# The loops of an attention and of two feed-forward passes written out, with every wait on a constant

## The reference

```python
# feed-forward: 8 experts of width 64, two picked per token, and a shared one of width 128
g = silu(einsum('th,ehi->tei', xf, w_gate))
u = einsum('th,ehi->tei', xf, w_up)
experts_y = einsum('tei,eih->teh', g * u, w_down)
...                                   # the two picked ones, weighed
shared = silu(x @ sw_gate) * (x @ sw_up) @ sw_down

# attention: 16 heads of 8 channels, power 4 of the scores in place of a softmax
s = einsum('bhtd,bhsd->bhts', q, k)
s = s - s.mean(-1)
s = s / (abs(s).mean(-1) + 1e-06) * score_gain
s = where(causal, s, -1000.0)
r = maximum(s, 0.0) ** 4
att = r / (r.sum(-1) + 1e-06)
y = einsum('bhts,bhsd->bhtd', att, v)
```

## Time and profile before

| what | us |
|---|---|
| runs | 505.57, 505.78, 507.81; median 505.78 |
| span of the profiled execution, first to last instruction (the profile gives no other time of it) | 505.4 |
| TensorE busy | 441.9 (87%) |
| VectorE busy | 402.7 (80%) |
| ScalarE busy | 342.0 (68%) |
| GpSimd busy | 243.8 (48%) |

### The profile page before, as it was taken

The page is one execution under the profiler, slowest core; times in us unless marked ns, Lnnn a source line. Parts: engine busy times, 40 slices in busy tenths (PEclk is TensorE's granted clock), DMA queues, the critical chain, the costliest instruction groups (busy, mean ns, idle before and its releaser), DMA issues. The chain is left out here.

```text
span 505.4 us, 8943 instructions
## 1 busy us (share of the span) xinstructions
PE 441.9 (87%) x2736; PEld 168.3 (33%) x2736; DVE 402.7 (80%) x832; ACT 342.0 (68%) x576; POOL 243.8 (48%) x180
## 2 busy tenths in 40 slices
PE   0879999664799999999999999999999995879996
PEld 0323444431232332333333322323323354334442
DVE  5884556976898998999989899989988969784443
ACT  3413223554999999999999999999989931523221
POOL 5940000333777686776877677676876720000000
PEclk9979999975999999999999999999999998799999
DMA  4300000025714205105114124043002300000001
GB/s 118 75 1 0 1 0 0 6 65 127 208 33 78 60 1 95 43 1 93 42 30 71 34 51 84 0 72 63 0 0 50 85 12 0 1 1 0 21 21 42
DMA packets 17796, 21.32 MB, mean 42 GB/s; under 512 B 4748, under 2 KB 10476, under 8 KB 17772
## 3 DMA queue, kind: packets, MB, share of 16 engines
q1 hardware_dynamic: 17452, 20.95, 19.2%
q10 hardware_dynamic: 320, 0.07, 0.1%
HBM read 13.02 MB, written 7.86 MB: 41 GB/s over the span
## 5 line engine op out<-in xcount | busy, mean ns | idle before, releaser
L1206 POOL TENSOR_TENSOR arena<-arena 128x1024 f32<-128x1024 f32 (+1 forms) x120 | 204.0, 1722 | 63.7 <-ACT arena L1178 63.5
L1136 DVE SCALAR_TENSOR_TENSOR arena<-bank,masks 128x1024 f32<-128x1024 f32 (+1 forms) x160 | 174.9, 1114 | 28.9 <-PE bank L1048 28.6
L1178 ACT ACTIVATE arena<-arena 128x1024 f32<-128x1024 f32 (+1 forms) x160 | 148.5, 961 | 8.8 <-DVE arena L1136 5.8
L1048 PE MATMUL bank<-Q,K 128*128 128x512 bf16 (+3 forms) x384 | 91.4, 334 | 10.6 <-DMA K<-k_parts 9.2
L1048 PE MATMUL bank<-K,Q 128*128 128x512 bf16 (+3 forms) x384 | 90.4, 331 | 11.6 <-DVE arena L1136 11.5
L1144 DVE TENSOR_SCALAR_CACHE_REDUCE bank<-bank 128x128 f32<-128x128 f32 (+7 forms) x128 | 94.8, 772 | 0.0
L1168 ACT ACTIVATE bank<-bank 128x128 f32<-128x128 f32 (+7 forms) x128 | 80.9, 632 | 8.9 <-PE bank L1048 8.6
L1079 PE MATMUL bank<-arena,Vq 128*32 128x512 f32 (+3 forms) x768 | 79.6, 495 | 0.0
L588 ACT ACTIVATE arena<-bank 128x512 f32<-128x512 f32 x40 | 23.9, 597 | 76.5 <-PE bank L463 76.5
L689 DVE TENSOR_TENSOR arena<-arena,bank 128x512 f32<-128x512 f32 x40 | 27.4, 686 | 42.8 <-PE bank L467 42.7
L1079 PE MATMUL bank<-arena,ones_rows 128*32 128x512 f32 (+3 forms) x640 | 61.1, 473 | 0.0
(11 more groups left out here) (122 smaller groups left out, 355.4 us busy)
## 6 DMA issues: line engine op xcount, KB each, us to landing
Q<-q_parts SPq DMA_DIRECT2D x24, 192.0 KB
att<-arena SPq DMA_DIRECT2D x28, 128.0 KB, 2.0
K<-k_parts SPq DMA_DIRECT2D x16, 128.0 KB
K<-k_parts SPq DMA_DIRECT2D x8, 192.0 KB
X<-in_L_attn_x SPq DMA_DIRECT2D x4, 256.0 KB, 4.6
K<-k_parts SPq DMA_DIRECT2D x16, 64.0 KB
out_x<-X SPq DMA_DIRECT2D x4, 256.0 KB, 2.3
q_parts<-arena SPq DMA_DIRECT2D x3, 256.0 KB
```

What stands on the lines that cost most here:

```text
L1048: last = nc.tensor.matmul(bank[:, lo + shift:hi + shift], left[par][:, g, blk * P:(blk + 1) * P], right[par][:, g, s0:s0 + hi - lo], start ...
L1136: nc.vector.scalar_tensor_tensor(Y(r, g)[:, lo - off(r):hi - off(r)], tiles[slot["lower", r, g]][:, lo:hi], 0.0, mask, ALU.max, ALU.mult). ...
L1178: nc.scalar.activation(z, Y(r, g)[:, tile_low(r) - off(r):T - off(r)], ACT.Square)\
L1206: nc.gpsimd.tensor_tensor(z, z, z, ALU.mult).then_inc(fourth_p, 1)
```

## The change

Four loops of the engines become loops of the program that builds the code, so that their bodies are written out: the spans 1 to 3 on TensorE, ScalarE and VectorE, in both passes, and the quads 1 to 6 on all five engines. The numbers of spans and quads are then known when the code is built, and all waits compare with constants. The work, its order on each engine and the semaphores stay.

```diff
             pe.wait_ge(wT_ready, NSPAN)
-            with pe.Fori(1, NSPAN) as i:
+            for i in range(1, NSPAN):
                 span(i, False)
...
                 take_weights(j)
-            with act.Fori(1, NSPAN) as i:
+            for i in range(1, NSPAN):
                 span(i, False)
...
             span(0, True)
-            with dve.Fori(1, NSPAN) as i:
+            for i in range(1, NSPAN):
                 span(i, False)
...
     def quads(engine, body):


-        body(0, 0, 1)
-        with engine.Fori(0, NQUAD // 2 - 1) as pair:
-            body(2 * pair + 1, 1, pair + 1)
-            body(2 * pair + 2, 0, pair + 2)
-        body(NQUAD - 1, 1, NQUAD // 2)
+        for q in range(NQUAD):
+            body(q, q % 2, q // 2 + 1)
```

## The result

The changed kernel takes 508.81 us in the median of 15 runs (507.38 to 511.17), the kernel before 506.57 us in the median of 15 runs (504.80 to 508.70). The ratio is 1.0052, with a 95% interval of 1.0039 to 1.0065: slower by about 2.6 us (2.0 to 3.3). The two medians alone lie 2.24 us apart (1.0044), inside that interval. The forecast was 507.8 us, which is 2.0 us more than the median known then (505.78), a ratio of 1.0040. The range held the time. But most of the chance (0.73) stood on a time within 0.5% of before, and the kernel is measured 0.52% slower.

A forecast was written before the change was run, and what follows sets the result against it. Attention was held bound by the TensorE-VectorE ring over PSUM tiles, feed-forward passes by TensorE. Waits add 2.6 us, entries give back 0.6: 2.0 more than the 505.78 median, 507.8 us, range 505.6 to 509.1.

The forecast's parts named there:

- The wait's place: VectorE's step in quads 1 to 6: `lower_ready` moves to a separate semaphore instruction, 0.43 us more per quad, 2.6 us.
- The upper bound of 0.53 per quad: Attention: if the ring also closes over quad 7's 0.10 us later start, six quads cost 3.2 us.
- The entries: TensorE entering both feed-forward loops: starts 0.05 us after ScalarE's last weight copy instead of 0.34, 0.6 us gained.
- Jumps and register work at nothing: Attention loop: sequencers do this while engines work on what was queued, so removing it gains nothing.
- Code fetch at nothing: Longer written-out program: fetching ahead costs nothing in straight code, since loop passes with and without fetches were equally long.
- rows 11: Profile rows cited for the loop's first pass: three 16 KB instruction packets between 192.3 and 227.9, none with jumps back.
- the line of half a per cent: Whole kernel: 2.5 us, about what a measurement can tell from no change, so slower begins at 508.3 us.
- its own range: Whole kernel: the forecast case's range, 507.2 to 508.5 us, with chance 0.65.
- The ring that pays at every hand-off: Attention, VectorE's last and next first step: also delayed, 0.53 x 6 = 3.2 us, 509.0 us in all; chance 0.13.
- quad 7's own slip: Attention: quad 7 was late for its own reason, so only the entries give, 505.2 us; chance 0.15.
- a code fetch exposed as a whole: Attention: four more quads pay for fetching code, 11.4 us, 519 us in all; chance 0.04.
- jumps that had cost: The three loops: six jumps back cost 0.95 us each, 5.7 us saved, waits free, 500 us; chance 0.03.

The follow-up runs named there:

- The pair of runs with the line moved: VectorE's wait on `lower_ready` put first in its step: in the changed kernel, 0.9969 of before; in the kernel before, loops kept, 1.0039.
- the spans alone: The kernel before with only the feed-forward span loops written out, the quads kept in their loop: 0.9990 of before.
- the run with two more instructions: The changed kernel with two more VectorE instructions (memsets) ahead of the quads: attention 0.32 us shorter than in the changed kernel.

## Why the prediction was right and wrong

- **The wait's place, 6 x 0.43 = 2.6 us: right.** Quads 1 to 5 measure 36.03 as forecast. From quad 0's start to quad 6's it adds 0.10 (quad 0, 35.05 to 35.15) and 5 x 0.43; quad 6 adds 0.33 beside its late step, since its interval had 0.10 already before. Together 2.6. The pair of runs with the line moved shows the cause: 35.60 written out with `lower_ready` first, 36.07 to 36.09 in the loop with it first.
- **The upper bound of 0.53 per quad: rightly not taken.** The 0.10 us at a quad's first step is there, and does not add up: the interval is 36.03, not 36.13. The late first step in the run with two more instructions shows why: 0.35 us at that place were made up within the quad.
- **The entries, 2 x 0.29 = 0.6 us: right.** TensorE starts 0.05 us after the last copy in place of 0.34, at both entries, in the kernel after and with the spans alone.
- **Jumps and register work at nothing: right.** With the wait moved, the written-out quads take 35.60, as in the loop.
- **Code fetch at nothing: the step that failed**, as far as is known. The prediction said that "fetching ahead costs nothing when the code is straight", from one pass of a loop whose quads were equally long. In the written-out code one step of quad 6 is late by 0.35 us, by its place in the code, and no other work covered it. That the delay is a fetch is inferred; that a place in straight code can cost 0.35 us on the path is shown, and the prediction had no term for it. It went by the packets of one queue and the length of quads (rows 11 leave out two packets on the second instruction queue, q14, in the same stretch), and did not ask whether a fixed place in the code can fall on a step that is waited for; where it falls cannot be read from the trace of before. With it the sum is 2.95 - 0.58 = 2.4 us, 0.47%.
- **The chances.** The forecast sum of 2.0 us lay 0.5 us below the line of half a per cent, and its own range went only 0.2 us over it; the term left out took most of that distance. The rest, from 2.4 to the measured 2.6, is inside the interval (2.0 to 3.3) and is not explained. The sum of what the profile shows, 1.0047, stands just under the line, the measured 1.0052 just over it, and the interval of 1.0039 to 1.0065 lies on both sides. So on which side the kernel came out is in part chance, and too much of the forecast was put on one of them.
- **The rivals.** The ring that pays at every hand-off and quad 7's own slip are ruled out by intervals of 36.03; a code fetch exposed as a whole (519) and jumps that had cost (500) by the times. Nine more packets came on q8 in the kernel after, and quads 1 to 5 are equally long beside them.

## What to carry to other kernels

Of several waits ahead of one instruction, put the one whose signal comes last where it stays on the instruction itself, and look in the built program at which one that is: in VectorE's step here the first in the code with constants, the last with registers. Before writing out a loop on a ring of hand-offs, ask what becomes of its waits, not only of its jumps. Where a forecast ends within half a microsecond of the line between "slower" and "no change", a single late step can decide, and the chances should say so.

## What was not expected of the hardware

- A signal that comes last and is met by a separate semaphore instruction on VectorE, not by the step itself, makes the quad 0.43 us longer (36.03 and 35.60). With four waits of TensorE for VectorE in a quad, that is about 0.1 us per hand-off, an estimate.
- A fixed place in VectorE's code delays one instruction by 0.35 us (0.40 us after its semaphore instruction in place of 0.045). Two places 384 recorded instructions apart behaved alike, and one or two instructions more ahead moved the delay to another step or hid it.
- Where the quads' loops jump back, no time is lost: 35.60 us with the jump and without, and 35.60 written out with the wait in its place.
